# QKV stage of a fused layer: the row statistics of a tile move to the end of VectorE's slot, and the wait for prepared weights moves to the first projection

## The chip, the cores and the metric

One Trainium2 chip, one core of it. The metric is the time of one execution in microseconds (us). The kernel before was run three times: 2370.19, 2377.79 and 2379.58 us.

## What is computed

The reference is one transformer layer on x of (2, 1024, 2048), in float32, followed by a dequantized 2048x2048 linear map. Only the first part is touched by the change:

```python
x = layernorm(hidden)                       # over the 2048 values of a row
y = einsum('blhc,hoc->bloh', x.reshape(b, l, 512, 4), W_read)   # 3 outputs
yn = (y - mean(y)) * rsqrt(var(y) + EPS) * gamma + beta
q, k, v = [yn[o] @ qkv_w[o].T for o in range(3)]
q, k = rope(q, pos), rope(k, pos)
```

After that come causal attention with 16 heads of 32, a gated write back to the residual, an MLP of the same kind and the final map. float32 products are made of three passes on split operands: `high` parts written by ScalarE, `low` parts (the rest) by VectorE.

## The kernel before

`build_qkv` works through 16 tiles of 128 rows. Each engine runs its own program: `steps` calls a `body` for slots s = 0, 1, 2, ..., written out for the first four slots, as a loop of two slots per pass from slot 4 on. In slot s an engine does pieces for several tiles at once: `live(0)` is tile s, `live(1)` tile s-1, and so on. Order inside an engine is the order of the code; between engines only semaphores count. The slot of each engine, before the change:

- SyncE's queue: writes `hs` of tile s-2 out (after ScalarE wrote it, L429 to L431), then loads tile s as `xt` (for TensorE) and `xc` (for VectorE and ScalarE), L437 and L438, then writes q and k of tile s-4.
- TensorE: `read` 0 and 1 (L575) for tile s-1; transposes of tile s-2, `turn_y(0)` and `turn_y(1)` (L562); `project(0)` (L589 to L593), which waits for the low part of the transposed tile; `turn_qk(0)` (L544); `read` 2 and 3; `turn_y(2)`; `project(1)`; `turn_qk(1)`; `project(2)`. Reads 2 and 3 write the same PSUM tile `psY` as reads 0 and 1, after VectorE has taken the first half out.
- VectorE: `lo_y(0)`, `lo_y(1)` (L628) of tile s-2, `less_mean(0)` (L641) of tile s-1, `x_statistics` (L653 to L661: four bn_stats over the row in `xc`, an aggregate, epsilon, negated mean, reciprocal) of tile s, `less_mean(1)` of tile s-1, `lo_y(2)`, the statistics of y (L681 to L694), the two rotary products `ra` and `rb` (L704, L707) of tile s-2, and `lo_qk` (L632) of tile s-3, twice.
- ScalarE: `hi_y` three times (L474), `first_norm` (L487 to L493, which writes `hs`), `hi_qk`, the square root for y (L507), the three normalized parts `yn` (L512), `hi_qk`, and the copy of v (L522). GpSimd adds `ra` and `rb` (L464).

In what follows "slot period" is the time from one `rb` product to the next. The weights are prepared inside the first slots: ScalarE scales and rounds them (`high_weights`, L351), VectorE makes the low parts (`low_weights`, L332, 12 operations at the start of slot 2), TensorE computes the bias rows in `psQ` (`bias_rows`, L370), VectorE splits them (L335, L337), and at the start of slot 2 TensorE waits for all of it before its reads:

```python
                    if at_slot(s, 2):
                        bias_rows(pe)
                        pe.wait_ge(act_w, O * KH)
                        pe.wait_ge(wl_ok, O * KH)
                        pe.wait_ge(brow_ok, 2)
```

Of the kernel before, what the change touches and what calls it, by code (L numbers as in the profile page):

```python
# [20 lines left out]
ACT = mybir.ActivationFunctionType  # L21
# [18 lines left out]
KD, KH, KM = D // P, H // P, M // P  # L40
# [178 lines left out]
def build_qkv(nc, io, k):  # L219
# [3 lines left out]
    with ExitStack() as ctx:  # L223
        sb, ps, sem = allocators(nc, ctx, "s1_")
        O = 3
# [3 lines left out]
        brow = sb("q_brow", [P, O * H], F32R)  # L229
# [10 lines left out]
        psQ = ps("psQ", [P, O, H])  # L240
# [15 lines left out]
        w_in, small_in, blk, dve_w, act_w, pe_w, d = (sem(n) for n in  # L256
            ("w_in", "small_in", "blk", "dve_w", "act_w", "pe_w", "d"))
# [69 lines left out]
        def low_weights(dve):  # L327
            for o in range(O):
                for kt in range(KH):
                    cols = slice(o * H, (o + 1) * H)  # L330
                    dve.wait_ge(act_w, o * KH + kt + 1)
                    dve.scalar_tensor_tensor(wl[:, kt, cols], wraw[:, kt, cols], gam[:, o, kt:kt + 1],  # L332
                                             wh[:, kt, cols], ALU.mult, ALU.subtract).then_inc(wl_ok, 1)
            dve.wait_ge(pe_w, 3)
            dve.tensor_copy(brow[:], psQ[:].rearrange("p o n -> p (o n)")).then_inc(brow_ok, 1)  # L335
            dve.wait_ge(brow_ok, 1)
            dve.tensor_tensor(brow[64:P, :], psQ[64:P].rearrange("p o n -> p (o n)"), brow[64:P, :],  # L337
                              ALU.subtract).then_inc(brow_ok, 1)

        def high_weights(act):  # L340
            act.wait_ge(small_in, 64)
            act.wait_ge(trig, 1)
            act.activation(sinT[:, :, 1, :], red[:], ACT.Sin)
            act.activation(sinT[:, :, 0, :], red[:], ACT.Sin, scale=-1.0).then_inc(trig, 1)
            act.wait_ge(trig, 3)
            act.activation(cosT[:], red[:], ACT.Sin).then_inc(trig, 1)
            act.wait_ge(w_in, 16)
            for o in range(O):
                for kt in range(KH):
                    cols = slice(o * H, (o + 1) * H)  # L350
                    act.activation(wh[:, kt, cols], wraw[:, kt, cols], ACT.Copy,  # L351
                                   scale=gam[:, o, kt:kt + 1]).then_inc(act_w, 1)

        def weight_sums(pe):
            pe.wait_ge(dve_w, 1)
# [9 lines left out]
        def bias_rows(pe):  # L365
            pe.wait_ge(dve_w, 2)
            pe.wait_ge(w_in, 16)
            for o in range(O):
                for kt in range(KH):
                    mm = pe.matmul(psQ[:, o, :], betb[:, o, kt, :], wraw[:, kt, o * H:(o + 1) * H],  # L370
                                   start=(kt == 0), stop=(kt == KH - 1))
            mm.then_inc(pe_w, 1)

        def at_slot(s, n):

            return s.reg is None and s.off == n
# [46 lines left out]
        with nc.Block() as block:  # L423
# [45 lines left out]
            def _(act):  # L469
# [23 lines left out]
                    act.activation(hs[:], xc[:, q], ACT.Identity, scale=sh[:, 0:1], bias=sh[:, 1:2]).then_inc(hs_ok, 1)  # L493

                def body(s, p, live):
                    if live(2):
                        hi_y(s, 0)
                        hi_y(s, 1)
# [28 lines left out]
            def _(pe):  # L527
# [66 lines left out]
                    mm.then_inc(qkv_mm, 1)  # L594

                def body(s, p, live):
                    if at_slot(s, 2):
                        bias_rows(pe)
                        pe.wait_ge(act_w, O * KH)
                        pe.wait_ge(wl_ok, O * KH)  # L600
                        pe.wait_ge(brow_ok, 2)
                    if live(1):
                        read(s, p, 0)
                        read(s, p, 1)
                    if live(2):
                        turn_y(s, 0)
                        turn_y(s, 1)
                        project(s, 0)
                    if live(3):
                        turn_qk(s, 0)  # L610
                    if live(1):
                        read(s, p, 2)
                        read(s, p, 3)
                    if live(2):
                        turn_y(s, 2)
                        project(s, 1)
                    if live(3):
                        turn_qk(s, 1)
                    if live(2):
                        project(s, 2)  # L620
# [4 lines left out]
            def _(dve):  # L625
# [4 lines left out]
                def lo_qk(s, r):  # L630
                    dve.wait_ge(qt_hi, count(s - 3, 2, r + 1))
                    dve.tensor_tensor(qtl[:, r], qk_bank[r][:], qth[:, r], ALU.subtract).then_inc(qt_lo, 1)  # L632
# [30 lines left out]
                def body(s, p, live):  # L663
                    if at_slot(s, 2):
                        low_weights(dve)
                        dve.wait_ge(trig, 4)
                    if live(2):
                        lo_y(s, 0)
                        lo_y(s, 1)
                    if live(1):  # L670
                        less_mean(s, 0)
                    if live(0):
                        x_statistics(s, p)
                    if live(1):
                        less_mean(s, 1)
                    if live(2):
# [33 lines left out]
                    if live(3):  # L710
                        lo_qk(s, 0)
                        lo_qk(s, 1)
                angles(dve)
                steps(dve, TILES, 3, 2, body)


# [1980 lines left out]
```

## Time and profile before

| | us |
|---|---|
| median of three runs | 2377.79 |
| lowest, highest | 2370.19, 2379.58 |
| the profiled execution, its own time | 2377.49 |
| span of its instructions | 2375.8 |
| TensorE busy in the span | 2200.8 |
| first to last `rb` product of slots 2 to 16 | 63.15 to 302.38 |

The span is the stretch from the first to the last instruction; 1.7 us lie around it. Times in the rows below are counted from its start. A row of a timeline gives start, duration, engine, line, operation, tiles and, in brackets, how long the engine was idle before it and what ended that. Starts of successive operations of one engine can lie closer than a duration, since they overlap a little. The QKV stage takes about the first 325 us; attention begins behind it.

### The profile page before, as it was taken

To read this page: it belongs to the slowest core of one execution; us is meant where nothing else is said; L and a number is where in the kernel's file an instruction comes from. 1 tells how busy PE (TensorE), PEld (TensorE's weight loads), DVE (VectorE), ACT (ScalarE), POOL (GpSimd) and SP (SyncE) were. 2 spreads that over 40 slices of the span, in tenths; PEclk is the share of its full clock that TensorE was granted. 3 is DMA by queue.
4 is the path that set the end of the run, shared out by engine and by line. 5 is a ranking of instruction groups with operands and counts; after the bars stand their busy time and mean duration, and the time that the engine had idled before them with its cause. 6 is when DMAs were issued, how large, how long until landed. Compare 5 with 4: busy or idle time off the path is not lost.

```text
span 2375.8 us, 34032 instructions
## 1 busy us (share of the span) xinstructions
PE 2200.8 (93%) x11560; PEld 1803.2 (76%) x11560; DVE 1333.3 (56%) x1744; ACT 1066.8 (45%) x1594; POOL 987.4 (42%) x613
## 2 busy tenths in 40 slices
PE   6999859999984999799999999998799999999999
PEld 5777736666653888688788899997678888888887
DVE  7778736777754888433333357677465265265322
ACT  3444426888883777621222346666322132122111
POOL 0111116999994778300000177873254153154110
PEclk9999967999997999899999999999899999999999
DMA  4777732333324666354553568778565465465443
GB/s 178 233 245 235 225 111 77 95 103 97 102 56 156 221 218 235 131 173 148 159 181 110 190 229 301 294 291 302 201 194 193 157 202 186 151 195 186 147 146 98
DMA packets 208614, 424.61 MB, mean 179 GB/s; under 512 B 16434, under 2 KB 131890, under 8 KB 181636
## 3 DMA queue, kind: packets, MB, share of 16 engines
q1 hardware_dynamic: 208516, 423.31, 54.2%
q8 instruction: 61, 1.00, 0.2%
q14 instruction: 37, 0.30, 0.0%
HBM read 284.31 MB, written 138.67 MB: 178 GB/s over the span
## 4 chain that ended last, share of the span: by engine, by line
PE 49%; DMA 8%; DVE 5%; ACT 3%; issue 2%; POOL 1%; SPq 1%; DVEq 0%; ACTq 0%
PE s_m_psG L2167 7%; PE s_m_psU L2167 7%; PE s_psF L2541 6%; PE s_psF L2543 6%; PE s_psF L2542 6%; PE s_w_psA L1751 5%; PE s_w_psB L1751 5%; DMA s_f_q<-wq 4%; DMA y<-s_f_xb 2%; PE s_w_psR L1268 1%; POOL s_f_q L2454 1%; PE s_w_psT L1783 1%; DVE s_w_ab L1529 1%; PE s_w_psB L1220 1%; DMA s_f_xl<-xnT 1%
## 5 line engine op out<-in xcount | busy, mean ns | idle before, releaser
L2541 PE MATMUL s_psF<-s_f_wh,s_f_xh 128*128 128x512 f32 x1024 | 402.3, 393 | 11.4 <-DVE s_f_xl L2420 6.6
L2543 PE MATMUL s_psF<-s_f_wh,s_f_xl 128*128 128x512 f32 x1024 | 400.2, 391 | 0.0
L985 POOL TENSOR_TENSOR s_a_pl<-s_a_pf,s_a_ph 128x1024 fp32r<-128x1024 f32 x128 | 302.0, 2391 | 22.6 <-ACT s_a_pf L950 22.5
L2416 ACT ACTIVATE s_f_xh<-s_f_xl 128x2048 fp32r<-128x2048 f32 x64 | 122.7, 1917 | 390.1 <-PE s_psF L2543 318.5
L895 DVE TENSOR_REDUCE s_a_mx<-s_psS 128x1 f32<-128x512 f32 (+7 forms) x256 | 185.1, 754 | 119.9 <-PE s_psS L825 119.5
L2514 POOL TENSOR_TENSOR s_f_xb<-s_f_xb,s_f_fb 128x512 f32<-128x512 f32 x64 | 98.8, 1543 | 358.5 <-DMA s_f_xb<-x 340.4
L2541 PEld LDWEIGHTS s_psF<-s_f_wh,s_f_xh 128*128 128x128 f32 x1024 | 193.6, 189 | 55.0 <-DVE s_f_xl L2420 9.5
L1919 POOL TENSOR_TENSOR s_w_yl<-s_w_y,s_w_yh 128x1024 fp32r<-128x1024 f32 x32 | 76.1, 2401 | 371.9 <-ACT s_w_yh L1831 371.9
L2543 PEld LDWEIGHTS s_psF<-s_f_wh,s_f_xl 128*128 128x128 f32 x1024 | 193.4, 189 | 40.9
L2420 DVE TENSOR_TENSOR s_f_xl<-s_f_xl,s_f_xh 128x2048 fp32r<-128x2048 f32 x64 | 161.2, 2519 | 80.9 <-ACT s_f_xh L2416 80.9
L2542 PE MATMUL s_psF<-s_f_wl,s_f_xh 128*128 128x512 f32 x512 | 201.2, 393 | 0.0
L947 ACT ACTIVATE s_a_ph<-s_psX 128x1024 fp32r<-128x1024 f32 (+1 forms) x160 | 150.6, 941 | 58.1 <-PE s_psX L851 54.4
L2454 POOL TENSOR_TENSOR s_f_q<-s_f_q,s_f_sz 128x512 f32<-128x512 f32 x48 | 115.2, 2419 | 135.5 <-DVE s_f_q L2449 135.5
L2485 DVE TENSOR_TENSOR s_f_xb<-s_psF,s_f_xb 128x512 f32<-128x512 f32 x64 | 43.9, 686 | 220.6 <-PE s_psF L2543 217.2
L817 PE MATMUL s_psS<-s_a_k,s_a_q 96*128 96x512 f32 (+3 forms) x384 | 124.3, 412 | 35.6 <-DVE s_a_mx L895 19.9
L464 POOL TENSOR_TENSOR s_q_qk<-s_q_ra,s_q_rb 128x1024 f32<-128x1024 f32 x16 | 37.8, 2360 | 277.9 <-DVE s_q_rb L707 277.9
L2542 PE MATMUL s_psF<-s_f_wl1a,s_f_xh 128*128 128x512 f32 x384 | 149.4, 389 | 0.0
L2227 DVE TENSOR_TENSOR s_m_mo<-s_m_psU,s_m_sil 128x512 f32<-128x512 f32 x64 | 44.2, 690 | 178.2 <-PE s_m_psU L2167 106.3
L869 PE MATMUL s_psO<-s_a_ph,s_a_vs 128*65 128x512 f32 (+3 forms) x384 | 128.8, 351 | 7.4 <-POOL s_a_pl L985 7.4
L950 ACT ACTIVATE s_a_pf<-s_psX 128x1024 f32<-128x1024 f32 x128 | 131.0, 1023 | 0.0
L869 PE MATMUL s_psO<-s_a_pl,s_a_vs 128*65 128x512 f32 (+3 forms) x384 | 125.5, 339 | 0.0
L2126 ACT ACTIVATE s_m_sil<-s_m_psG 128x512 f32<-128x512 f32 x64 | 38.1, 595 | 167.7 <-PE s_m_psG L2167 167.7
(310 smaller groups left out, 5674.3 us busy)
## 6 DMA issues: line engine op xcount, KB each, us to landing
s_f_xl<-xnT SPq DMA_DIRECT2D x64, 1024.0 KB, 5.7
s_q_xt<-xT SPq DMA_DIRECT2D x16, 1024.0 KB, 7.5
s_q_xc<-xP SPq DMA_DIRECT2D x16, 1024.0 KB, 9.5
hsD<-s_q_hs SPq DMA_DIRECT2D x16, 1024.0 KB, 4.8
s_w_hin<-hsD SPq DMA_DIRECT2D x16, 1024.0 KB, 4.9
hs<-s_w_res SPq DMA_DIRECT2D x16, 1024.0 KB, 3.9
s_m_raw<-giT SPq DMA_DIRECT2D x32, 512.0 KB, 4.4
mlpT<-s_m_mo SPq DMA_DIRECT2D x64, 256.0 KB, 2.4
```

The lines of the kernel that those rows point to most:

```text
L869: mm = pe.matmul(psO[0:VW, half, 512 - n:512], vs[:, r, ki, :], part[:, r, at:at + n], start=(ki == 0 and part is ph), stop=(ki == (3, 7)[ ...
L895: dve.tensor_reduce(mx[:, slot % 2, qi:qi + 1], psS[:, off:off + (qi + 1) * P], AX, ALU.max).then_inc(mx_ok, 1)
L947: act.activation(ph[:, r, at:at + wide[j]], src, ACT.Exp, scale=scale).then_inc(exp_ok, 1)
L950: act.activation(full, src, ACT.Exp, scale=scale).then_inc(exp_ok, 1)
L985: pool.tensor_tensor(pl[:, r, cols], pf[:, j - 1], ph[:, r, cols], ALU.subtract).then_inc(pl_ok, 1)
L1751: mm = pe.matmul(bank[:, 0:n], a[:, p, kt], b[:, kt, cols], start=False, stop=(kt == KM - 1 and a is yl))
L2167: mm = pe.matmul(bank[u % 2][:], a[:, kt], b[:, :, kt], start=(i == 0 and a is w[m][0] and b is xh), stop=(i == KH - 1 and a is w[m][1]))
L2420: dve.tensor_tensor(xl[u % 3][:], xl[u % 3][:].bitcast(F32), xh[:, u % 2], ALU.subtract).then_inc(x_lo, 1)
L2454: pool.tensor_tensor(w[:, n % 4], w[:, n % 4], sz[:, n // 4 % 2, 0], ALU.mult).then_inc(w_ok, 1)
L2541: pe.matmul(out[:], xh[:, u % 2, kt], high(c, kt), start=(kt == 0), stop=False)
L2542: pe.matmul(out[:], xh[:, u % 2, kt], low(c, kt), start=False, stop=False)
L2543: mm = pe.matmul(out[:], xl[u % 3][:, kt], high(c, kt), start=False, stop=(kt == KD - 1))
```

## The change

Four edits in `build_qkv`:

1. VectorE does `x_statistics` of tile s at the end of slot s, behind `lo_qk`, not between the two halves of `less_mean`. In slot 1 it is left out, and tile 1's statistics come in slot 2 behind `low_weights`.
2. TensorE's three waits for prepared weights stand directly ahead of `project(0)` of slot 2, behind reads 0 and 1 and two transposes.
3. `bias_rows` is issued in slot 1, behind reads 2 and 3, which is the same place in TensorE's order.
4. The rounded copy of the bias rows is made by ScalarE (`bias_high`, at the start of slot 2), not by VectorE.

```diff
--- before.py
+++ after.py
@@ -331,8 +331,6 @@
                     dve.wait_ge(act_w, o * KH + kt + 1)
                     dve.scalar_tensor_tensor(wl[:, kt, cols], wraw[:, kt, cols], gam[:, o, kt:kt + 1],
                                              wh[:, kt, cols], ALU.mult, ALU.subtract).then_inc(wl_ok, 1)
-            dve.wait_ge(pe_w, 3)
-            dve.tensor_copy(brow[:], psQ[:].rearrange("p o n -> p (o n)")).then_inc(brow_ok, 1)
             dve.wait_ge(brow_ok, 1)
             dve.tensor_tensor(brow[64:P, :], psQ[64:P].rearrange("p o n -> p (o n)"), brow[64:P, :],
                               ALU.subtract).then_inc(brow_ok, 1)
@@ -350,6 +348,10 @@
                     cols = slice(o * H, (o + 1) * H)
                     act.activation(wh[:, kt, cols], wraw[:, kt, cols], ACT.Copy,
                                    scale=gam[:, o, kt:kt + 1]).then_inc(act_w, 1)
+
+        def bias_high(act):
+            act.wait_ge(pe_w, 3)
+            act.activation(brow[:], psQ[:].rearrange("p o n -> p (o n)"), ACT.Copy).then_inc(brow_ok, 1)
 
         def weight_sums(pe):
             pe.wait_ge(dve_w, 1)
@@ -493,6 +495,8 @@
                     act.activation(hs[:], xc[:, q], ACT.Identity, scale=sh[:, 0:1], bias=sh[:, 1:2]).then_inc(hs_ok, 1)
 
                 def body(s, p, live):
+                    if at_slot(s, 2):
+                        bias_high(act)
                     if live(2):
                         hi_y(s, 0)
                         hi_y(s, 1)
@@ -594,21 +598,24 @@
                     mm.then_inc(qkv_mm, 1)
 
                 def body(s, p, live):
-                    if at_slot(s, 2):
-                        bias_rows(pe)
-                        pe.wait_ge(act_w, O * KH)
-                        pe.wait_ge(wl_ok, O * KH)
-                        pe.wait_ge(brow_ok, 2)
                     if live(1):
                         read(s, p, 0)
                         read(s, p, 1)
+                    if at_slot(s, 1):
+                        read(s, p, 2)
+                        read(s, p, 3)
+                        bias_rows(pe)
                     if live(2):
                         turn_y(s, 0)
                         turn_y(s, 1)
+                        if at_slot(s, 2):
+                            pe.wait_ge(act_w, O * KH)
+                            pe.wait_ge(wl_ok, O * KH)
+                            pe.wait_ge(brow_ok, 2)
                         project(s, 0)
                     if live(3):
                         turn_qk(s, 0)
-                    if live(1):
+                    if live(1) and not at_slot(s, 1):
                         read(s, p, 2)
                         read(s, p, 3)
                     if live(2):
@@ -663,14 +670,13 @@
                 def body(s, p, live):
                     if at_slot(s, 2):
                         low_weights(dve)
+                        x_statistics(s - 1, 1 - p)
                         dve.wait_ge(trig, 4)
                     if live(2):
                         lo_y(s, 0)
                         lo_y(s, 1)
                     if live(1):
                         less_mean(s, 0)
-                    if live(0):
-                        x_statistics(s, p)
                     if live(1):
                         less_mean(s, 1)
                     if live(2):
@@ -710,6 +716,8 @@
                     if live(3):
                         lo_qk(s, 0)
                         lo_qk(s, 1)
+                    if live(0) and not at_slot(s, 1):
+                        x_statistics(s, p)
                 angles(dve)
                 steps(dve, TILES, 3, 2, body)
 
```

VectorE in slot 3 before, from `lo_y(0)` on (`ytl` is the low part of the transposed tile, `yr` what `less_mean` writes, `bst` and `sx` the row statistics):

```order
L628 TENSOR_TENSOR s_q_ytl<-s_psA,s_q_yth 128x512 [waits s1_yt_hi]
L628 TENSOR_TENSOR s_q_ytl<-s_psB,s_q_yth 128x512 [waits s1_yt_hi]
L641 SCALAR_TENSOR_TENSOR s_q_yr<-s_q_wsum,s_q_sx,s_psY 128x768 [waits s1_yn_ok,s1_y_mm,s1_x_norm]
L653 BN_STATS s_q_bst<-s_q_xc 128x6 [waits s1_x_in1]
L653 BN_STATS s_q_bst<-s_q_xc 128x6 x3
L656 BN_AGGR s_q_sx<-s_q_bst 128x2 [waits s1_x_norm]
L658 TENSOR_SCALAR s_q_sx<-s_q_sx 128x1 [waits s1_x_norm]
L659 TENSOR_SCALAR s_q_sx<-s_q_sx 128x1
L661 RECIPROCAL s_q_sx<-s_q_sx 128x1 [waits s1_x_norm]
L641 SCALAR_TENSOR_TENSOR s_q_yr<-s_q_wsum,s_q_sx,s_psY 128x768 [waits s1_yn_ok,s1_y_mm,s1_x_norm]
```

and now, from `lo_qk` of slot 3 (`qtl`) to `lo_y(0)` of slot 4; the branch is the entry into the loop:

```order
L639 TENSOR_TENSOR s_q_qtl<-s_psC,s_q_qth 128x512 [waits s1_qt_hi]
L639 TENSOR_TENSOR s_q_qtl<-s_psB,s_q_qth 128x512 [waits s1_qt_hi]
L660 BN_STATS s_q_bst<-s_q_xc 128x6 [waits s1_x_in1]
L660 BN_STATS s_q_bst<-s_q_xc 128x6 x3
L663 BN_AGGR s_q_sx<-s_q_bst 128x2 [waits s1_x_norm]
L665 TENSOR_SCALAR s_q_sx<-s_q_sx 128x1 [waits s1_x_norm]
L666 TENSOR_SCALAR s_q_sx<-s_q_sx 128x1
L668 RECIPROCAL s_q_sx<-s_q_sx 128x1 [waits s1_x_norm]
L86 UNCONDITIONAL_BRANCH
L86 ISA
L635 TENSOR_TENSOR s_q_ytl<-s_psA,s_q_yth 128x512 [waits s1_yt_hi]
```

The six rows of the statistics went from between `yr` and `yr` to between `qtl` and the next slot's `ytl`; the same holds in every later slot up to 15.

TensorE before, from the bias rows (`wraw`, `betb`) to the first projection (`brow`) of slot 2:

```order
L370 MATMUL s_psQ<-s_q_wraw,s_q_betb 128x512 [waits s1_w_in,s1_dve_w]
L370 MATMUL s_psQ<-s_q_wraw,s_q_betb 128x512 x11
L575 MATMUL s_psY<-s_q_spf,s_q_xt 128x96 [waits s1_x_in1,s1_brow_ok,s1_y_norm,s1_wl_ok,s1_act_w]
L575 MATMUL s_psY<-s_q_spf,s_q_xt 128x96 x7
L562 MATMUL s_psA<-c_ident,s_q_yn 128x128 [waits s1_yn_ok]
L562 MATMUL s_psA<-c_ident,s_q_yn 128x128 x3
L562 MATMUL s_psB<-c_ident,s_q_yn 128x128 [waits s1_yn_ok]
L562 MATMUL s_psB<-c_ident,s_q_yn 128x128 x3
L589 MATMUL s_psQ<-s_q_brow,s_q_c 128x512 [waits s1_yt_lo,s1_yt_hi]
```

and now:

```order
L372 MATMUL s_psQ<-s_q_wraw,s_q_betb 128x512 [waits s1_w_in,s1_dve_w]
L372 MATMUL s_psQ<-s_q_wraw,s_q_betb 128x512 x11
L579 MATMUL s_psY<-s_q_spf,s_q_xt 128x96 [waits s1_y_norm,s1_x_in1]
L579 MATMUL s_psY<-s_q_spf,s_q_xt 128x96 x7
L566 MATMUL s_psA<-c_ident,s_q_yn 128x128 [waits s1_yn_ok]
L566 MATMUL s_psA<-c_ident,s_q_yn 128x128 x3
L566 MATMUL s_psB<-c_ident,s_q_yn 128x128 [waits s1_yn_ok]
L566 MATMUL s_psB<-c_ident,s_q_yn 128x128 x3
L593 MATMUL s_psQ<-s_q_brow,s_q_c 128x512 [waits s1_yt_hi,s1_brow_ok,s1_yt_lo,s1_wl_ok,s1_act_w]
```

No instruction moved; the waits for `brow_ok`, `wl_ok` and `act_w` went from the first read to the first projection.

## Rows read from the trace of the kernel before

**Rows 1.** Page, part 1: busy us, share of the span and instructions of each engine.

```profile
PE 2200.8 (93%) x11560; PEld 1803.2 (76%) x11560; DVE 1333.3 (56%) x1744; ACT 1066.8 (45%) x1594; POOL 987.4 (42%) x613
```

**Rows 2.** Waits, 60 to 300 us: who waited for what: us in total, times, longest.

```profile
DVE s_q_bst L653 <- DMA s_q_xc<-xP: 26.7, 13, 3.5
...
DVE s_q_yr L641 <- PE s_psY L575: 1.3, 2, 0.9
```

**Rows 3.** VectorE timeline: start, us, what; first and last of 15 `rb` products.

```profile
63.15 1.22 DVE L707 TENSOR_TENSOR s_q_rb<-s_psQ,s_sinT 128x1024 f32<-128x1024 f32 x1
...
302.38 1.21 DVE L707 TENSOR_TENSOR s_q_rb<-s_psQ,s_sinT 128x1024 f32<-128x1024 f32 x1
```

**Rows 4.** VectorE timeline, one long slot, in brackets the idle time before.

```profile
165.75 1.22 DVE L707 TENSOR_TENSOR s_q_rb<-s_psQ,s_sinT 128x1024 f32<-128x1024 f32 x1
...
167.48 0.68 DVE L632 TENSOR_TENSOR s_q_qtl<-s_psB,s_q_qth 128x512 fp32r<-128x512 f32 x1
...
168.93 0.69 DVE L628 TENSOR_TENSOR s_q_ytl<-s_psA,s_q_yth 128x512 fp32r<-128x512 f32 x1 [0.78 <-ACT s_q_yth L474]
...
174.73 2.47 DVE L653 BATCH_NORM_STATS2 s_q_bst<-s_q_xc 128x6 f32<-128x512 f32 x4 [3.51 <-DMA s_q_xc<-xP]
...
178.00 1.01 DVE L641 SCALAR_TENSOR_TENSOR s_q_yr<-s_q_wsum,s_q_sx,s_psY 128x768 f32<-128x768 f32 x1
...
184.23 1.22 DVE L707 TENSOR_TENSOR s_q_rb<-s_psQ,s_sinT 128x1024 f32<-128x1024 f32 x1
```

**Rows 5.** VectorE timeline, in the short slot before it.

```profile
156.06 2.47 DVE L653 BATCH_NORM_STATS2 s_q_bst<-s_q_xc 128x6 f32<-128x512 f32 x4 [0.38 <-DMA s_q_xc<-xP]
...
159.34 1.01 DVE L641 SCALAR_TENSOR_TENSOR s_q_yr<-s_q_wsum,s_q_sx,s_psY 128x768 f32<-128x768 f32 x1
```

**Rows 6.** TensorE timeline, the same short slot.

```profile
153.63 0.49 PE L589 MATMUL s_psQ<-s_q_brow,s_q_c 128*128 128x512 f32 x1 [0.30 <-DVE s_q_ytl L628]
...
157.21 1.92 PE L575 MATMUL s_psY<-s_q_spf,s_q_xt 128*128 128x96 f32 x16
...
167.67 0.60 PE L562 MATMUL s_psA<-c_ident,s_q_yn 128*128 128x128 f32 x4
...
169.89 0.49 PE L589 MATMUL s_psQ<-s_q_brow,s_q_c 128*128 128x512 f32 x1 [0.96 <-DVE s_q_ytl L628]
```

**Rows 7.** TensorE and VectorE timelines, slot with slow clock, 218 to 230 us.

```profile
218.38 0.60 PE L562 MATMUL s_psA<-c_ident,s_q_yn 128*128 128x128 f32 x4
...
221.51 0.79 PE L589 MATMUL s_psQ<-s_q_brow,s_q_c 128*128 128x512 f32 x1 [0.30 <-DVE s_q_ytl L628]
...
226.56 1.92 PE L575 MATMUL s_psY<-s_q_spf,s_q_xt 128*128 128x96 f32 x16
...
228.52 1.01 DVE L641 SCALAR_TENSOR_TENSOR s_q_yr<-s_q_wsum,s_q_sx,s_psY 128x768 f32<-128x768 f32 x1 [0.94 <-PE s_psY L575]
```

**Rows 8.** Windows: busy us by engine (PE, PEld, DVE, ACT, POOL), granted clock, DMA, GB/s.

```profile
46.00:52.00 6.00, 5.15 (x25) 4.90 (x25) 0.99 (x2) 1.20 (x2) 0.00 (x0) 0.61 0.00 0
306.75:310.15 3.40, 3.40 (x10) 2.65 (x9) 0.18 (x1) 0.00 (x0) 0.00 (x0) 0.50 0.83 231
```

**Rows 9.** Timeline of the first slots, VectorE and TensorE.

```profile
26.34 2.47 DVE L653 BATCH_NORM_STATS2 s_q_bst<-s_q_xc 128x6 f32<-128x512 f32 x4 [1.74 <-DMA s_q_xc<-xP]
...
41.96 1.75 DVE L335 CAST s_q_brow<-s_psQ 128x1536 fp32r<-128x1536 f32 x1
...
43.74 1.76 DVE L337 TENSOR_TENSOR s_q_brow<-s_psQ,s_q_brow 64x1536 fp32r<-64x1536 f32 x1
...
51.85 0.47 PE L589 MATMUL s_psQ<-s_q_brow,s_q_c 128*128 128x512 f32 x1 [0.85 <-DVE s_q_ytl L628]
...
56.98 1.01 DVE L641 SCALAR_TENSOR_TENSOR s_q_yr<-s_q_wsum,s_q_sx,s_psY 128x768 f32<-128x768 f32 x1 [0.52 <-PE s_psY L575]
```

**Rows 10.** ScalarE: timeline row of the `hs` write; group row of the page.

```profile
160.81 2.10 ACT L493 ACTIVATE s_q_hs<-s_q_xc,s_q_sh 128x2048 f32<-128x2048 f32 x1
...
L950 ACT ACTIVATE s_a_pf<-s_psX 128x1024 f32<-128x1024 f32 x128 | 131.0, 1023 | 0.0
```

## The prediction

> **What bounds the kernel now.** The page says that TensorE is busy for 93% of the span [rows 1], but that is a mean over all stages and the change touches one. So I read the QKV stage by itself, first the waits, then the timelines. In the waits VectorE stands for 26.7 us, 13 times, before the row statistics until the tile's row copy `xc` has landed, and only 1.3 us until TensorE's reads are done [rows 2]. The stage's pace is the time from one `rb` product to the next: 15 of them from 63.15 to 302.38, so 14 slot periods of (302.38 - 63.15) / 14 = 17.09 us [rows 3]. They alternate. In the long one, 165.75 to 184.23, VectorE waits 3.51 us for `xc` [rows 4]; in the short one before it, which ends at 165.75, it waits 0.38 [rows 5]. Shorts are about 15.7 us, longs about 18.3.
>
> What the reader should see next is where the statistics lie. In the short slot TensorE starts projection 0 at 153.63 and its second reads at 157.21 [rows 6]: the second `less_mean` cannot start before those reads are done. VectorE does the statistics (156.06 to 159.34, 3.28 us) in just this hole [rows 5]. So a row copy that is in time makes them nearly free today; only a late one costs.
>
> **The ring after the change.** Behind the change the order on VectorE is `rb`, two `lo_qk`, statistics, `lo_y(0)`, and TensorE's projection 0 waits for `lo_y(0)`. That closes a ring, whose links all have rows:
>
> - projection 0 to second reads: 157.21 - 153.63 = 3.58 [rows 6]
> - second reads to second `less_mean`, where that did wait for TensorE: 228.52 - 226.56 = 1.96 [rows 7]
> - second `less_mean` to `rb`: 165.75 - 159.34 = 6.41 [rows 4, 5]; the long slot has 6.23 [rows 4]
> - `rb` to the start of the last `lo_qk`: 167.48 - 165.75 = 1.73 [rows 4], and about 0.60 to the next start
> - statistics: 3.28 [rows 5]
> - start of `lo_y(0)` to projection 0: 169.89 - 168.93 = 0.96 [rows 4, 6]
>
> The sum is 18.5 us. Every slot is then as long as a long one is today. The wait for `xc` does go: the copy lands 174.73 - 162.91 = 11.8 us after `hs` is written [rows 4, 10], and with the statistics at the slot's end VectorE asks for it some 10 us later than now. But it is replaced by 3.28 us on the ring. In its place VectorE will idle about 4 us before the second `less_mean`, waiting for TensorE. Cost: 14 x (18.5 - 17.09) = **+19.7 us**. Bounds: with 63.15 - 56.98 = 6.17 for the third link [rows 3, 9] the ring is 18.3 (+16); with 0.3 us for the loop's branch and register instructions, which now stand right ahead of `lo_y(0)` and are hidden by a wait today, it is 18.8 (+24).
>
> **TensorE's clock.** Between the transposes into `psA` and projection 0 TensorE does next to nothing. Of 15 such stretches, seven are 1.9 to 2.2 us long, as 167.67 to 169.89 [rows 6], and after none is the clock low. Eight are 2.9 to 3.1 us, as 218.38 to 221.51 [rows 7], and in three of these the granted clock falls to 0.50 (1.2 GHz) around the start of the projection; the last is at 306.75 [rows 8]. Then projection 0 to second reads takes 226.56 - 221.51 = 5.05 us [rows 7] and not 3.58, so 1.5 us more, and this link is on the new ring. After the change the stretch has the same work in it, but it lasts until the statistics and `lo_y(0)` are done: TensorE's own work between two projections 0 is 167.67 - 153.63 = 14.04 us up to the transposes, so 18.5 - 14.04 = 4.45 us. From none of seven at 2.1 and three of eight at 3.05, a straight line reaches nearly all at 4.45. I take 13 of 14 slots at 1.3 us, below 1.5 because some of the slow time falls on the idle part: **+17 us**. Bounds: three falls (+4.5), or 14 at 1.5 (+21).
>
> The Trainium skill ("TensorE: Matmul & The Clock Gate", section "HAM oscillation — how this bites in real kernels") speaks against this change in the same sense: a loop in which TensorE waits in every pass drops to the half clock again in every pass, and pays each time. By that rule alone the sum would have +21 here in place of +17, by today's rate of falls +4.5; three of 15 slots in this trace bear the rule out so far.
>
> **The start.** In slot 1 the second `less_mean` no longer stands behind the statistics, which waited 1.74 us for their copy [rows 9]; it starts when the reads end, 1.1 us earlier, and `low_weights` with it, so it ends at 40.9 and not near 42. The bias rows are in `psQ` by then. ScalarE's copy of 128x1536 costs some 1.5 us (estimate from 1023 ns for 128x1024 out of PSUM [rows 10]) in place of VectorE's 1.75, and is done at 41.4. The low part, 1.76 [rows 9], ends at 43.2, the statistics of tile 1 at 46.4, and projection 0 starts at 47.4 and not at 51.85 [rows 9]. TensorE's reads and transposes are done well before, since they don't wait any more; but it has then idled some 5 us, so the projection runs at the half clock: second `less_mean` at 47.4 + 5.05 + 1.96 = 54.4 against 56.98 [rows 9]. The gain at the first `rb` is **-2.3 us** (bounds: 0 and -4). The new place of `bias_rows` changes nothing: no instruction of TensorE moves.
>
> **The end.** Slots 16 and 17 have no statistics and stay as they are. Attention starts when the last q and k are out, so the delay passes on whole.
>
> **Sum.** +19.7 + 17 - 2.3 = +34.4. The profiled execution took 2377.49, close to the median of 2377.79, so 2377.5 + 34.4 = **2412 us**.
>
> **Rivals.**
>
> A. The clock falls as seldom as today. For: five of eight 3-us stretches pass without it. Against: the new stretch is 1.4 us longer and is there in each slot. 19.7 + 4.5 - 2.3 = +22: 2399 us.
>
> B. The clock stays low for a second stretch in many slots, as it does around 46 to 52, at 0.61 in the mean [rows 8]. Then a slot loses some 2.8 us: 14 x 2.8 = 39; 19.7 + 39 - 2.3 = +57: 2434 us. Against: the three falls in the steady slots were each over before the second reads (their 16 matmuls took 1.92 us in the slow-clock slot as in the other [rows 6, 7]).
>
> C. Faster: the wait for the row copy was the bound and nothing replaces it. Then all slots are short: 14 x (15.7 - 17.09) - 2.3 = -22: 2356 us. This decides itself at projection 0: if `lo_y(0)` were late for another reason by at least 3.28 us, the statistics would be hidden in front of it. Today VectorE is idle only 0.78 us there [rows 4].
>
> D. About the same. The links come from different slots and needn't add up: at 0.2 us under my lower bound, 18.1, with no fall and the start at its best, it is 14 - 4 = +10: 2388 us.
>
> That the change doesn't do what it says is excluded by the order of VectorE's instructions.
>
> **How the numbers follow.** Main case 0.56 (2412), A 0.20 (2399), D 0.10 (2388), B 0.08 (2434), C 0.06 (2356). A measurement of this kernel can tell a difference of about 0.5%, 12 us. Faster by more: 0.06 (C). Within: 0.10 (D). Slower: 0.84 (main, A, B). The range takes in the main case, A and their bounds, the ring at its lower bound with the start at its best and no fall (16 - 4 = +12) and at 18.8 with a fall in each slot (+43), and leaves out C, part of D and most of B: 2390 to 2426.
>
> **What would show it.** VectorE's wait for `xc` gone; a wait of about 4 us before the second `less_mean` (L648 in the new file) for TensorE's reads in every slot; `rb` every 19.5 to 20 us without alternation; a low granted clock in nearly each slot and 5 us from projection 0 to the second reads; the first `rb` near 61. The prediction is wrong if `lo_y(0)` isn't what projection 0 waits for, or if second reads start less than 3.5 us after it.

## The result, and the profile after

The changed kernel took 2403.59 us, median of four runs (2399.93 to 2412.68), against 2373.99 for the kernel before in the same comparison (four runs, 2359.23 to 2379.58). The ratio is 1.0147, with a 95% interval of 1.0119 to 1.0176. A second comparison on another occasion (f1 below) gave 1.0148 (1.0129 to 1.0167). So the change makes the kernel slower by about 1.5%, some 30 to 35 us (the two medians are 29.6 us apart, the ratio stands for 35). The profiled execution took 2412.68 with a span of 2410.8.

The page's first part hardly shows it. TensorE's share of the span fell by one point against [rows 1]:

```profile
PE 2215.6 (92%) x11560; PEld 1818.5 (75%) x11560; DVE 1329.1 (55%) x1743; ACT 1068.6 (44%) x1595; POOL 989.7 (41%) x613
```

The waits of the QKV stage, 55 to 340 us, do show it (us in total, times, longest):

```profile
DVE s_q_yr L648 <- PE s_psY L579: 66.3, 12, 5.8
...
PE s_psQ L593 <- DVE s_q_ytl L635: 41.3, 12, 3.7
```

VectorE's 26.7 us of waiting for the row copy [rows 2] are gone; no row of the answer names it. The wait of VectorE for TensorE's second reads, 1.3 us before, is 66.3, and TensorE waits 41.3 us for the low part ahead of projection 0. The first and the last of the 15 `rb` products of slots 2 to 16, to be set beside [rows 3] (VectorE timeline):

```profile
59.89 1.21 DVE L713 TENSOR_TENSOR s_q_rb<-s_psQ,s_sinT 128x1024 f32<-128x1024 f32 x1
...
333.41 1.22 DVE L713 TENSOR_TENSOR s_q_rb<-s_psQ,s_sinT 128x1024 f32<-128x1024 f32 x1
```

14 periods take 333.41 - 59.89 = 273.52 us, 19.54 each, against 17.09. At the `rb` of slot 16 the changed kernel is 333.41 - 302.38 = 31.0 us behind, and at that of slot 17 (346.80 against 315.76) still 31.0. That is the whole of the result, within the scatter of the runs. The traced execution lost another 4 us behind the stage; what lies behind it differs by up to 18 us from trace to trace (last section).

One slot on VectorE, as [rows 4] (VectorE timeline):

```profile
195.81 1.21 DVE L713 TENSOR_TENSOR s_q_rb<-s_psQ,s_sinT 128x1024 f32<-128x1024 f32 x1
...
197.54 0.68 DVE L639 TENSOR_TENSOR s_q_qtl<-s_psB,s_q_qth 128x512 fp32r<-128x512 f32 x1
...
198.14 2.46 DVE L660 BATCH_NORM_STATS2 s_q_bst<-s_q_xc 128x6 f32<-128x512 f32 x4
...
201.24 0.16 DVE L668 RECIPROCAL s_q_sx<-s_q_sx 128x1 f32<-128x1 f32 x1
...
201.75 0.69 DVE L635 TENSOR_TENSOR s_q_ytl<-s_psA,s_q_yth 128x512 fp32r<-128x512 f32 x1 [0.35 <-issue]
...
209.76 1.02 DVE L648 SCALAR_TENSOR_TENSOR s_q_yr<-s_q_wsum,s_q_sx,s_psY 128x768 f32<-128x768 f32 x1 [5.79 <-PE s_psY L579]
...
216.23 1.22 DVE L713 TENSOR_TENSOR s_q_rb<-s_psQ,s_sinT 128x1024 f32<-128x1024 f32 x1
```

The statistics start 0.60 us behind the last `lo_qk`, with no wait for their copy, and end 3.3 us later; only then comes `lo_y(0)`. The second `less_mean` (209.76) is preceded by 5.79 us of idle time, which ends with TensorE's reads. TensorE in two slots (timeline: transposes into `psA`, projection 0, second reads):

```profile
197.94 0.60 PE L566 MATMUL s_psA<-c_ident,s_q_yn 128*128 128x128 f32 x4
...
202.68 0.50 PE L593 MATMUL s_psQ<-s_q_brow,s_q_c 128*128 128x512 f32 x1 [3.68 <-DVE s_q_ytl L635]
...
207.79 1.92 PE L579 MATMUL s_psY<-s_q_spf,s_q_xt 128*128 128x96 f32 x16
...
222.69 0.50 PE L593 MATMUL s_psQ<-s_q_brow,s_q_c 128*128 128x512 f32 x1 [3.27 <-DVE s_q_ytl L635]
...
226.27 1.92 PE L579 MATMUL s_psY<-s_q_spf,s_q_xt 128*128 128x96 f32 x16
```

and the granted clock in two stretches from projection 0 to the second reads, as [rows 8] (windows):

```profile
142.03:147.13 5.10, 5.10 (x17) 4.06 (x18) 1.28 (x2) 0.00 (x0) 0.00 (x0) 0.67 0.99 333
...
222.69:226.27 3.58, 3.58 (x18) 2.93 (x18) 1.28 (x2) 0.00 (x0) 0.00 (x0) 1.00 1.06 366
```

From the transposes at 197.94 to projection 0 at 202.68 are 4.74 us. This projection took 207.79 - 202.68 = 5.11 us to the second reads; the one at 222.69 took 3.58. In the first window the clock was at its lower level, 1.2 GHz, for two thirds of the time (0.67 in the mean), in the second at 2.4 GHz throughout. Of the 14 slots that end at the `rb` of slots 3 to 16, ten are of the first kind (5.04 to 5.12 us) and four of the second. The stretch ahead of projection 0 was 4.3 to 4.8 us long in 13 of the 14 slots and 3.3 in the first. Its length doesn't tell the two kinds apart: it was 4.43 us ahead of the slow projection at 142.03 and 4.44 ahead of the fast one at 222.69.

The start, as [rows 9] (VectorE and TensorE timelines: low part of the bias rows, statistics of tile 1, `lo_y(0)`, projection 0, second `less_mean`):

```profile
41.23 1.76 DVE L335 TENSOR_TENSOR s_q_brow<-s_psQ,s_q_brow 64x1536 fp32r<-64x1536 f32 x1
...
43.02 2.47 DVE L660 BATCH_NORM_STATS2 s_q_bst<-s_q_xc 128x6 f32<-128x512 f32 x4
...
46.33 0.69 DVE L635 TENSOR_TENSOR s_q_ytl<-s_psA,s_q_yth 128x512 fp32r<-128x512 f32 x1
...
47.16 0.77 PE L593 MATMUL s_psQ<-s_q_brow,s_q_c 128*128 128x512 f32 x1 [5.06 <-DVE s_q_ytl L635]
...
53.71 1.01 DVE L648 SCALAR_TENSOR_TENSOR s_q_yr<-s_q_wsum,s_q_sx,s_psY 128x768 f32<-128x768 f32 x1 [5.17 <-issue]
```

### The profile page after: what moved, and what is told of

Read it like the earlier page. It is cut to its first block, busy times and chain, and to the rows that moved or that the text cites. A ratio compares the mean times of both kernels' runs of the same rounds, so it can differ in the third digit from the quotient of the medians.

```text
span 2410.8 us, 34032 instructions
## 1 busy us (share of the span) xinstructions
PE 2215.6 (92%) x11560; PEld 1818.5 (75%) x11560; DVE 1329.1 (55%) x1743; ACT 1068.6 (44%) x1595; POOL 989.7 (41%) x613
## 4 chain that ended last, share of the span: by engine, by line
PE 54%; DMA 4%; DVE 4%; ACT 3%; issue 2%; POOL 1%; SPq 1%; DVEq 0%; ACTq 0%; POOLq 0%
PE s_psF L2549 8%; PE s_psF L2550 8%; PE s_psF L2551 8%; PE s_m_psG L2175 7%; PE s_m_psU L2175 7%; PE s_w_psA L1759 4%; PE s_w_psB L1759 4%; PE s_w_psR L1276 2%; DMA s_f_q<-wq 2%; PE s_w_psT L1791 1%; DMA y<-s_f_xb 1%; DVE s_w_ab L1537 1%; PE s_w_psB L1228 1%; DMA s_f_xl<-xnT 1%; PE s_w_psT L1776 1%
## 5 line engine op out<-in xcount | busy, mean ns | idle before, releaser
L2551 PEld LDWEIGHTS s_psF<-s_f_wh,s_f_xl 128*128 128x128 f32 x1024 | 193.4, 189 | 40.3
L2550 PEld LDWEIGHTS s_psF<-s_f_wl,s_f_xh 128*128 128x128 f32 x512 | 97.2, 190 | 20.0
```

The lines of the kernel that those rows point to most:

```text
L2550: pe.matmul(out[:], xh[:, u % 2, kt], low(c, kt), start=False, stop=False)
L2551: mm = pe.matmul(out[:], xl[u % 3][:, kt], high(c, kt), start=False, stop=(kt == KD - 1))
```

## The experiments

The theory: (a) the statistics now lie on a ring through projection 0, (b) that makes TensorE idle long enough for its clock to fall, and (c) in the old place they were hidden but for a late copy. The rival: the other three edits cost the time. "Stage" is the time of the `rb` of slot 17, with 315.76 us for the kernel before and 346.80 for the changed one.

### e1: the statistics back in their place, all else as changed

```diff
-                        x_statistics(s - 1, 1 - p)
...
                         less_mean(s, 0)
+                    if live(0):
+                        x_statistics(s, p)
...
-                    if live(0) and not at_slot(s, 1):
-                        x_statistics(s, p)
```

> The changed kernel with edit 1 undone: the row statistics lie again between the two halves of less_mean; the waits for weights and the bias copy on ScalarE stay as changed. Ring theory (the statistics on the way from rb to projection 0 cost 1.3 us a slot, the slow clock of TensorE another 1.1): the slots are those of before again, 14 periods of 17.1 us with the wait for the row copy of some 27 us, and only the start's gain of 2 to 3 us is left, so about 3 us faster than before. Rival (the start edits or ScalarE's copy cost the time): still 20 us or more slower than before.

Measured: ratio to before 0.9996 (0.9978 to 1.0014). The first and last `rb` of slots 2 to 16 (VectorE timeline), and VectorE's wait for the copy (waits, 60 to 300 us):

```profile
56.40 1.22 DVE L714 TENSOR_TENSOR s_q_rb<-s_psQ,s_sinT 128x1024 f32<-128x1024 f32 x1
...
292.96 1.22 DVE L714 TENSOR_TENSOR s_q_rb<-s_psQ,s_sinT 128x1024 f32<-128x1024 f32 x1
```

```profile
DVE s_q_bst L660 <- DMA s_q_xc<-xP: 26.0, 13, 3.2
```

Periods of (292.96 - 56.40) / 14 = 16.90, with 26.0 us of waits for the copy, as before. The 30 us are gone with edit 1, so the rival falls. The trace shows a start that is 6.7 us earlier than [rows 3], more than forecast, and 3.5 us earlier than in the changed kernel. Two things make the 3.5: projection 0 of slot 2 starts at 45.09 and not at 47.16, with tile 1's statistics back in slot 1, and it gets through to the second reads in 3.12 us, not in 4.53. The stage ends at 306.36, 9.4 us earlier than before. The medians show 1.5 us of that, and the interval of the ratio (5 us faster to 3 slower) leaves 9.4 out. The traced execution of before took 2377.49 us and stood above the median of before in this comparison (2364.31), and the traced execution of e1 was the fastest of its ten (2357.52), so the 9.4 us come from one trace on either side; why so little of it arrives stays open.

### e2: the statistics at the slot's end, all else as before

```diff
                     if at_slot(s, 2):
                         low_weights(dve)
+                        x_statistics(s - 1, 1 - p)
...
-                    if live(0):
-                        x_statistics(s, p)
...
                         lo_qk(s, 1)
+                    if live(0) and not at_slot(s, 1):
+                        x_statistics(s, p)
```

> The kernel before with edit 1 alone: statistics at the end of VectorE's slot, the weights as before. Ring theory: periods of 19.5 us as in the changed kernel, second less_mean waits 4 to 6 us for TensorE in each slot, 31 to 38 us slower than before, since the start's gain is missing and the statistics of tile 1 come on top. Rival (start edits cost it): within 10 us of before.

Measured: ratio 1.0164 (1.0139 to 1.0189), 2404.65 against 2364.31 us. The first and last `rb` (VectorE timeline):

```profile
63.82 1.22 DVE L706 TENSOR_TENSOR s_q_rb<-s_psQ,s_sinT 128x1024 f32<-128x1024 f32 x1
...
340.66 1.21 DVE L706 TENSOR_TENSOR s_q_rb<-s_psQ,s_sinT 128x1024 f32<-128x1024 f32 x1
```

Periods of 19.77 us, eleven slots with a slow projection 0. The medians are 40.3 us apart, a little over the expected 31 to 38. The stage is 38.3 us longer than before. Edit 1 alone is the loss, and the other three give about 7 us of it back (354.06 against 346.80 at slot 17).

### e3, f1 and f2: TensorE kept busy in its idle stretch

```diff
                         turn_y(s, 1)
+                        if (s - 3).exists():
+                            for _ in range(12):
+                                pe.matmul(psC[:].rearrange("p a b -> p (a b)"), c64[:], brow[:, 0:H], start=True, stop=True)
```

> The changed kernel with 12 extra products of 128x512 (about 0.23 us each, 2.8 us in all, results overwritten unread) that TensorE does in its idle stretch ahead of projection 0, from slot 3 on. Ring and clock theory: the stretch has room for them, the clock no longer falls, projection 0 to second reads is 3.58 us in all slots in place of 5.1 in ten of them, periods 18.4 to 18.9, so 14 to 16 us faster than the changed kernel and 14 to 20 slower than before. Rival (the clock's share is hidden, the ring alone costs 30 us): time as changed, or slower by the extra work.

Measured: ratio to before 1.0112 (1.0086 to 1.0138), 2392.80 against 2364.31 us, so 28 us slower than before where 14 to 20 was expected. In its trace no projection 0 from slot 3 to slot 16 is slow (3.47 to 3.58 us), and the `rb` of slot 17 is at 333.51. Since the changed kernel had been timed on another occasion, both were run again side by side:

> The changed kernel once more, beside the filled one on the same chip. The stage: first rb at 59.9, periods of 18.4 us without and 19.9 with a fall of the clock, and 0.5 more in every second slot (the loop's branch), nine to thirteen falls in 14 slots; 1.3 to 1.6% slower than before. The slots 2 to 16 of the first trace took 273.5 us.

> The kernel with 12 extra products again, now beside the changed one: if the clock is worth 1.5 us per fall, 13 to 17 us faster than it on the same chip, with the same periods of 18.4 and 18.9 and no fall in the stage. If the first comparison (8 us by the ratios, from different chips) holds on one chip too, part of the stage's gain is lost behind the stage.

Measured: the changed kernel 2400.39 us (ratio 1.0148, 1.0129 to 1.0167), the filled one 2389.45 (1.0105, 1.0083 to 1.0127), so 10.9 us faster with more work. TensorE in one slot of f2 (timeline: transposes into `psB`, the extra products, projection 0, second reads):

```profile
209.65 0.63 PE L566 MATMUL s_psB<-c_ident,s_q_yn 128*128 128x128 f32 x4
...
210.04 2.99 PE L613 MATMUL s_psC<-s_q_brow,s_q_c 128*128 128x512 f32 x12
...
213.56 0.49 PE L593 MATMUL s_psQ<-s_q_brow,s_q_c 128*128 128x512 f32 x1 [0.53 <-DVE s_q_ytl L638]
...
217.12 1.92 PE L579 MATMUL s_psY<-s_q_spf,s_q_xt 128*128 128x96 f32 x16
```

The clock from 60 to 300 us (windows), first the changed kernel, then the filled one:

```profile
60.00:300.00 240.00, 198.17 (x1117) 168.10 (x1115) 163.13 (x329) 99.50 (x161) 30.76 (x13) 0.94 0.67 211
```

```profile
60.00:300.00 240.00, 231.64 (x1337) 195.83 (x1336) 171.55 (x350) 104.31 (x169) 30.98 (x13) 1.00 0.71 223
```

The extra products take the stretch from 210.04 to 213.03; projection 0 waits for VectorE all the same and then runs at full clock, 217.12 - 213.56 = 3.56 us to the second reads. The mean clock goes from 0.94 to 1.00. The periods are 18.36 and 18.89 in turn. The stage is 346.74 - 332.23 = 14.5 us shorter. The expected 13 to 17 us for the whole kernel were missed: 10.9 arrive in the medians and 10.0 in the spans (2392.8 and 2382.8), and the rest is lost behind the stage. So in the stage the falls of the clock are worth ten times 1.5 us, and what remains is the ring.

The two alternating periods are a surprise that this pair makes plain. In the loop, every second slot is preceded by its branch and register instructions. In the changed kernel [0.35 <-issue] stands before `lo_y(0)` at 201.75, and the same operation 20 us earlier started with no such gap: from the start of the reciprocal to that of `lo_y(0)` are 201.75 - 201.24 = 0.51 us there and 0.10 here (181.33 to 181.43). So the branch costs 0.4 us in every second slot; the other 0.1 of the difference lies between the second `less_mean` and `rb` (6.48 and 6.38 us in f2). In the old order `lo_y(0)` waited for ScalarE [rows 4], which hid most of it (e4 below keeps 0.1, 16.34 and 16.23 us in turn from projection 0 to projection 0).

### e4: in the old place, and the row copy loaded first

```diff
-                        sp.dma_start(xt[:, p], io["xT"][:, :, ds(tok, P)]).then_inc(x_in[p], 16)
-                        sp.dma_start(xc[:, p], io["xP"][ds(tok, P), :]).then_inc(x_in[p], 16)
+                        sp.dma_start(xc[:, p], io["xP"][ds(tok, P), :]).then_inc(c_in[p], 16)
+                        sp.dma_start(xt[:, p], io["xT"][:, :, ds(tok, P)]).then_inc(x_in[p], 16)
```

It is e1 otherwise, and each reader waits for its own semaphore.

> Statistics back in their place as in e1, and the row copy xc is loaded ahead of xt with a semaphore of its own, so that the statistics wait for it alone. Ring theory (what costs in the kernel before is only that the copy is late in every second slot): the copy lands 2 to 3 us earlier, long slots shrink from 18.3 to about 16, waits for the copy from 27 us to under 8, 12 to 20 us faster than before. Rival (the transfer's time is set by the writes ahead of it, or TensorE is the bound at 17 us a slot): the copy lands as late or the wait moves to TensorE, under 5 us faster than before.

Measured: ratio 0.9943 (0.9921 to 0.9965), 2352.70 against 2364.31. The copy's time from issue to landing in the kernel before and in e4 (DMA issues, 63 to 290 us; count, size, median us):

```profile
s_q_xc<-xP SPq DMA_DIRECT2D x13, 1024.0 KB, 9.6
```

```profile
s_q_xc<-xP SPq DMA_DIRECT2D x12, 1024.0 KB, 6.8
```

It lands 2.8 us sooner, `xt` in its turn later (9.3 us, 7.6 before), and no engine waits for either in the steady slots. The periods are 16.21 in the mean, the stage ends at 296.65, 19.1 us earlier than before. Of these 9.4 are e1's. What the load's new place brings is the difference to e1, 306.36 - 296.65 = 9.7 us in the stage and 10 in the medians of the same comparison (2362.80 and 2352.70). So 26 us of waits are gone and the stage is 9.7 us shorter: a late copy was all that the statistics cost in the old place, but another ring lay close beneath. The medians are 11.6 us faster than before, just under the expected 12 to 20. The order of the loads and the semaphore of their own were not tried one without the other. What bounds the slot now (VectorE: `lo_y(0)`, second `less_mean`; then TensorE: transposes into `psA`, projection 0; timelines):

```profile
173.11 0.69 DVE L636 TENSOR_TENSOR s_q_ytl<-s_psA,s_q_yth 128x512 fp32r<-128x512 f32 x1 [1.06 <-ACT s_q_yth L477]
...
179.57 1.01 DVE L649 SCALAR_TENSOR_TENSOR s_q_yr<-s_q_wsum,s_q_sx,s_psY 128x768 f32<-128x768 f32 x1 [1.07 <-PE s_psY L580]
```

```profile
171.76 0.60 PE L567 MATMUL s_psA<-c_ident,s_q_yn 128*128 128x128 f32 x4
...
174.03 0.49 PE L594 MATMUL s_psQ<-s_q_brow,s_q_c 128*128 128x512 f32 x1 [1.22 <-DVE s_q_ytl L636]
```

It is TensorE's own 14.04 us [rows 6] plus the 2.27 us from 171.76 to 174.03 (2.20 in every second slot), in which ScalarE and VectorE make the two parts of the transposed tile.

### b0: the kernel before, traced again

> The kernel before, unchanged, for a second trace: how far its stage differs from execution to execution. The copy's wait seems to have two patterns (before: 3.3 and 0.5 us in turn, e1: 1.9 us in each slot). Expected: first rb at 63.2, periods of 16.9 to 17.1 us in either pattern; the rest of the kernel, from the rb of slot 17 to the end, between 2049 and 2064 us as in the six traces so far.

Its `rb` products run from 65.19 to 303.84, 17.05 a period, with waits for the copy of 3.1 and 0.8 us in turn, and slot 17 comes at 315.70. The rest, to the end of the span, is 2059.8 us. The stage is as long; the start scatters by 2 us, and this is the clock too: projection 0 of slot 2 starts at 52.04 and takes 4.96 us to the second reads, in the first trace it starts at 51.85 and takes 3.11. In slot 17 it is the other way round: there the first trace has a fall [rows 8] and this one has none, so that the two are level again.

### e5: the same late statistics, 1.2 us further on

```diff
                     if live(2):
                         lo_y(s, 0)
                         lo_y(s, 1)
+                    if live(1) and not at_slot(s, 1):
+                        x_statistics(s - 1, 1 - p)
                     if live(1):
                         less_mean(s, 0)
...
                         lo_qk(s, 1)
-                    if live(0) and not at_slot(s, 1):
-                        x_statistics(s, p)
```

Tile 0's statistics stay in slot 0, and tile 1's come in slot 2 at the new place, not behind `low_weights`.

> The changed kernel with the statistics of a tile not at the end of its slot but 1.2 us later, at the start of the next one, behind lo_y(0) and lo_y(1) and ahead of the first half of less_mean. Same VectorE work, same late moment for the row copy, but projection 0 no longer stands behind it. Ring theory: the 3.28 us lie beside projection 0 (3.1 us), only about 1 us of them delays the second reads, so periods of 16.3 to 16.6 us, no fall of the clock, no wait for the row copy, 8 to 13 us faster than before and some 40 faster than the changed kernel. Rival (VectorE has too much work wherever the statistics lie, or the late statistics delay hs and the loads): periods of 18 us or more.

Measured: ratio 0.9998 (0.9977 to 1.0019), no gain on before where 8 to 13 us was expected, and 1.5% (some 35 us) faster than the changed kernel by the ratios. The `rb` of slot 17 is at 313.44, 2.3 us earlier than before. The periods are 17.46 and not 16.3 to 16.6. VectorE (`lo_y(0)`, statistics, both halves of `less_mean`) and TensorE (projection 0, second reads) in one slot (timelines):

```profile
182.72 0.69 DVE L635 TENSOR_TENSOR s_q_ytl<-s_psA,s_q_yth 128x512 fp32r<-128x512 f32 x1 [1.07 <-ACT s_q_yth L476]
...
183.93 2.46 DVE L660 BATCH_NORM_STATS2 s_q_bst<-s_q_xc 128x6 f32<-128x512 f32 x4
...
187.31 1.01 DVE L648 SCALAR_TENSOR_TENSOR s_q_yr<-s_q_wsum,s_q_sx,s_psY 128x768 f32<-128x768 f32 x1
...
190.44 1.01 DVE L648 SCALAR_TENSOR_TENSOR s_q_yr<-s_q_wsum,s_q_sx,s_psY 128x768 f32<-128x768 f32 x1 [2.12 <-PE s_psY L579]
```

```profile
183.65 0.50 PE L593 MATMUL s_psQ<-s_q_brow,s_q_c 128*128 128x512 f32 x1 [1.22 <-DVE s_q_ytl L635]
...
188.38 1.80 PE L579 MATMUL s_psY<-s_q_spf,s_q_xt 128*128 128x96 f32 x14 [0.98 <-DVE s_q_yr L648]
```

Projection 0 starts 0.93 us behind `lo_y(0)`, as in the theory, there is no slow projection in any slot, and no wait for the copy. But the second reads wait 0.98 us for the first half of `less_mean`, so projection 0 to second reads is 4.73 us and not 3.58. My expectation added this 1.15 to VectorE's ring of about 15.4; it belongs to the ring of e4 over TensorE, 14.04 + 2.20 + 1.15 = 17.39 (17.46 with 2.27). The theory stands, and one link of the estimate was wrong. The same 3.3 us of VectorE work on the same late data cost 2.1 us a slot (19.54 against 17.46) by standing ahead of `lo_y(0)` and not behind it; 1.0 of it is the ring (18.47 in f2 against 17.46), the rest the clock.

### e6: the waits for weights alone

```diff
                         bias_rows(pe)
-                        pe.wait_ge(act_w, O * KH)
-                        pe.wait_ge(wl_ok, O * KH)
-                        pe.wait_ge(brow_ok, 2)
...
                         turn_y(s, 1)
+                        if at_slot(s, 2):
+                            pe.wait_ge(act_w, O * KH)
+                            pe.wait_ge(wl_ok, O * KH)
+                            pe.wait_ge(brow_ok, 2)
                         project(s, 0)
```

> The kernel before with TensorE's waits for weights at the first projection alone (edits 2 and 3), the bias copy on VectorE as before. Splits the start's gain: reads and transposes no longer follow the last weight, so projection 0 comes some 4.3 us earlier (45.7 against 51.85 less the time of two lo_y and hi_y), first rb at 59 to 60 in place of 63.15; the rest of the start's gain in e1 is then ScalarE's copy and the bias rows' place.

This is edit 2 alone; `bias_rows` keeps its place in slot 2, which is the same place in TensorE's order as edit 3's. Measured: one run of 2358.43 us. Projection 0 of slot 2 (TensorE timeline):

```profile
47.28 0.47 PE L589 MATMUL s_psQ<-s_q_brow,s_q_c 128*128 128x512 f32 x1 [4.66 <-DVE s_q_ytl L629]
```

It comes at 47.28 and not at 51.85 or, in b0, 52.04; the first `rb` is at 60.13 and the stage ends at 310.78, 5.0 us before either trace of the kernel before. In e1 the first `rb` is at 56.40, another 3.7 us earlier. Of these, 2.2 are the earlier projection 0 (45.09 against 47.28), which the bias copy on ScalarE brings; the other 1.5 are the clock, for this projection takes 4.66 us to the second reads in e6 and 3.12 in e1. One trace of each doesn't tell whether that belongs to the edit.

### e7: the transposes ahead of the reads

e4, with `turn_y(0)` ahead of `read` 0 and 1:

```diff
+                    if live(2):
+                        turn_y(s, 0)
                     if live(1):
                         read(s, p, 0)
                         read(s, p, 1)
...
                     if live(2):
-                        turn_y(s, 0)
                         turn_y(s, 1)
```

> As e4, and turn_y(0) ahead of reads 0 and 1 on TensorE. In e4 the ring goes over TensorE: transposes into psA, ScalarE's high part, VectorE's low part, projection 0, 2.2 us in which TensorE idles. With the reads (1.76 us) put into this hole projection 0 starts 0.7 to 0.9 us earlier in each slot: periods of 15.4 to 15.7 in place of 16.2, 7 to 11 us faster than e4, 18 to 28 faster than before. Rival (VectorE's own 14 us and its wait for the second reads bound the slot at 16.2): same as e4.

Measured: ratio 0.9885 (0.9862 to 0.9908), 2340.86 against 2369.51 us, so 1.15% faster than before; with the changed kernel at 1.0148 (f1, against the kernel before as run beside it), the two are 2.6% of before apart, about 62 us. Against e4 the stage is 296.65 - 284.39 = 12.3 us shorter. TensorE (timeline: transposes into `psA`, reads, transposes into `psB`, projection 0) and the first and last `rb` (VectorE timeline):

```profile
163.49 0.60 PE L567 MATMUL s_psA<-c_ident,s_q_yn 128*128 128x128 f32 x4
...
163.93 1.92 PE L580 MATMUL s_psY<-s_q_spf,s_q_xt 128*128 128x96 f32 x16
...
165.69 0.61 PE L567 MATMUL s_psB<-c_ident,s_q_yn 128*128 128x128 f32 x4
...
166.59 0.49 PE L594 MATMUL s_psQ<-s_q_brow,s_q_c 128*128 128x512 f32 x1 [0.29 <-DVE s_q_ytl L637]
```

```profile
55.10 1.21 DVE L716 TENSOR_TENSOR s_q_rb<-s_psQ,s_sinT 128x1024 f32<-128x1024 f32 x1
...
271.01 1.21 DVE L716 TENSOR_TENSOR s_q_rb<-s_psQ,s_sinT 128x1024 f32<-128x1024 f32 x1
```

The reads now lie in the stretch in which TensorE idled for the low part. The periods are (271.01 - 55.10) / 14 = 15.42, and the stage ends at 284.39, 31.4 us earlier than before. This is the best version of this study.

## Why the prediction was right, and where it was off

The forecast was 2412 us (+34), the result 2403.59: +29.6 us by the medians, +35 in the traced execution, and +31.0 at the end of the stage. 3.5 us of the miss in absolute time are the base: the sum started from 2377.5, and the median of before in the comparison is 2373.99. Step by step, in the stage:

| term | forecast | measured |
|---|---|---|
| ring without a slow clock | 18.5 us, +19.7 | f2: (318.14 - 59.62) / 14 = 18.47, +19.3 |
| slow projections | 13 x 1.3 = +17 | 10 x 1.5 = +15 |
| start | -2.3 | 59.89 - 63.15 = -3.3 |
| sum at slot 16 | +34.4 | +31.0 |

- **Where the statistics lie.** Right. Their place behind `lo_qk` put all 3.3 us between `rb` and projection 0, and e1, e2 and e5 show that this place decides. The hole in which they were hidden is still there, empty: VectorE idles up to 5.8 us before the second `less_mean`. I had said about 4; with a slow projection it is 5.8, without 4.3.
- **The ring's links.** Right. The forecast's add up to 18.52; a slot without branch and slow clock took 18.37 (f2). The loop's branch, which I kept as a bound of 0.3, took 0.4 in every second slot. These two small errors, and a first period of only 17.12 us in f2, offset each other. I had said that `rb` would come without alternation; the periods run from 16.83 (the first) to 20.42 us, by branch and clock.
- **The clock.** Right in kind and in the price of a fall; the number was too high, and that it came so near was in part luck. A straight line from 3 of 8 stretches gave 13 of 14 slots; 10 fell, the same ten in f1. Each took the full 1.5 us from projection 0 to the second reads, so my reduction to 1.3 for a part in idle time was not needed. The measured 4.3 to 4.8 us of idle stretch in 13 slots match the forecast 4.45. But the 3 of 8 was a high draw: in e1, e6 and b0 a fall followed in only 3 of 26 stretches of 2.8 to 3.1 us (1 of 11, 1 of 7, 1 of 8). By my estimate the same line drawn through these would have given some 4 slots and +6 us, close to rival A. That longer stretches fall more often is shown; the line is not, nor why ten slots fall and four of them don't. By the Trainium skill ("TensorE: Matmul & The Clock Gate", section "HAM oscillation — how this bites in real kernels") a fall would have come in every pass; the traces have it in ten of 14.
- **The start.** The reads no longer wait, projection 0 starts at 47.16 (forecast 47.4) and runs partly at the slow clock; it got through in 4.53 us, not 5.05. So the second `less_mean` comes at 53.71 and not at 54.4, 0.7 us earlier. The other 0.3 is my own: 56.98 - 54.4 is 2.6, and I put down 2.3. In b0 the start is itself 2 us later than in [rows 9].
- **Rivals.** In absolute time A (few falls, 2399) was nearer than the main case: seven of the eight executions of the changed kernel took 2395 to 2404 us. By the difference to before (+29.6 against +22 and +34) and by the traces, with ten falls and not three, it was the main case. The range's upper end, 2426, is 5 us above what its own terms give (2377.5 + 43 = 2420.5); the result doesn't hang on it. C (nothing replaces the wait) is what e4 shows for an early copy in the old place: 16.2 us a slot, and 15.4 only when TensorE's own ring is shortened.

## What to carry to other kernels

A wait that is seen in one place tells that data come late, not that the work should be moved behind it: before moving it, look what the old place hid (here 3.3 us of statistics under a projection) and who waits behind the new place. The late data can be had earlier at its source; swapping two loads and giving each a semaphore of its own brought about 0.5% (e4 against e1), where moving the consumer cost 1.5%. The sum of the waits doesn't tell what that is worth: 26 us of them went and 9.7 us were gained, since the next ring was only 0.7 us a slot shorter. And a pause of TensorE that repeats in each slot can be paid twice, in the pause and in the slower matmuls behind it, if those are on the way to the next slot: here in ten slots of 14, 15 us beside the ring's 19.

## What the runs showed that was not expected

- A loop's branch and register instructions cost VectorE 0.4 us a pass when it comes to them at work (0.51 against 0.10 us ahead of `lo_y(0)`), and little where it would wait behind them anyway (e4, from projection 0 to projection 0: 16.34 and 16.23 us in turn).
- Adding 180 unread products of 128x512 (12 in each of slots 3 to 17) to TensorE made the kernel 10.9 us faster.
- What lies behind the stage scatters: from slot 17's `rb` to the end of the span the twelve traces have 2046 to 2064 us, for the same instructions, and the changed kernel alone has both ends (2064.0, and 2046.1 in f1). It isn't attention, whose last VectorE instruction (`s_a_ot`) comes 399.1 to 400.1 us behind that `rb` in all twelve. From there to the first `mo` product of the MLP, the gated write, the changed kernel takes 1040.62 - 746.45 = 294.2 us in its first trace and 1026.07 - 746.26 = 279.8 in f1, which is 14.4 of the 17.9 us. TensorE's clock differs in this stretch, 0.89 against 0.97 (windows, first trace, then f1):

```profile
800.00:985.00 185.00, 178.45 (x1155) 158.34 (x1156) 151.96 (x237) 136.23 (x334) 132.12 (x128) 0.89 0.58 205
```

```profile
800.00:985.00 185.00, 175.75 (x1236) 153.70 (x1236) 162.25 (x254) 146.23 (x360) 142.97 (x137) 0.97 0.64 228
```

- Part of a stage's gain doesn't reach the end: 9.4 us in e1's stage are 1.5 in the medians, 19.1 are 11.6 in e4, 14.5 are 10.9 in f2. The scatter behind the stage makes single traces poor witnesses of it; whether a shorter stage also lengthens what follows wasn't settled.
